# A macaron block (expert feed-forward, state-space mixer, expert feed-forward): named activation table sets, fewer paced scatters, and sums of squares moved from VectorE to ScalarE

## The chip, the cores and the metric

One core of a Trainium2 chip runs the whole kernel as one launch. TensorE multiplies matrices, VectorE, ScalarE and GpSimd (POOL in the profile) work elementwise, SyncE (SP) issues transfers, and GpSimd issues the indirect ones. Each engine runs its own instruction list strictly in order and meets the others at semaphores. The metric is the time of one execution on the device in microseconds, the median of the runs.

## The reference, cut to what matters

```python
x = x + 0.5 * _L0_ffn_ref(_layernorm(x), ...)      # shared expert plus the best 2 of 8 experts
x = x + _L0_attn_ref(_layernorm(x), ...)           # the mixer, below
x = x + 0.5 * _L0_ffn_ref(_layernorm(x), ...)
# in the mixer, x is (4, 1024, 128), D_INNER = 256, 4 heads, 16 states
zxbcdt = x @ in_proj_w.T
xBC = silu(conv4(xBC)); u, Bm, Cm = split(xBC)
Bm = Bm / (norm(Bm) + EPS);  Cm = Cm / (norm(Cm) + EPS)
dt = softplus(dt_raw + dt_bias)
S = 1.0 / (1.0 + dt**2 * A)
w = S * (w - dt * A * ys + dt * Bu);  ys = ys + dt * w;  o = ys . C_t      # scan over tokens
h = x + (y * silu(z)) @ out_proj_w.T
v = mean(h * h);  hn = h * rsqrt(v + EPS) * norm2_w
ffn = silu(hn @ gate_w.T) * (hn @ up_w.T) @ down_w.T
```

## The kernel before, in words

There are 4096 tokens, four sequences of 1024, cut in 8 blocks of 512, two to a sequence. The kernel has three parts. The first feed-forward takes the span up to 230 us, the mixer follows up to about 580 us, and the second feed-forward goes to the end.

A feed-forward norms the tokens, chooses two experts for each, and scatters its rows into one region per expert in HBM (`pool_scatter`, one indirect transfer of 128 rows at a time, 8 for a block, line L716). Then it runs the experts over tiles of 128 rows (`pe_experts` and its partners), and scatters the answers back.

The recurrence of the mixer is turned into decays and rotations: the scan over tokens becomes an exponential of running sums of logarithms (`log_sums`) times sines of running sums of an arctangent (`arctan`, `phase_sums`, `sine_args_c`, `sine_c`), so that chunks of 32 tokens can be multiplied on TensorE (`make_gram`, `state_sum`, `outputs`).

The mixer is software-pipelined by hand. Each engine has a function `body(at)` which lists its steps, and `in_order` calls it for n = -8, -7 and on; `at(-5)` is the block whose number is n - 5, or nothing. One call is a turn here. The order in `body` is the order on the engine; nothing reorders it. On ScalarE (L954 on) a turn before is: `theta` (block k), `hnt_copy`, `root`, `sine_c`, `h_start`, `sine_b`, `inverse_ln`, `inverse_exp`, two `silu_gate`, `c_places`, the third `silu_gate`, `silu_u`, `silu_z`, `silu_bc`, `tm_copy` 0, `silu_z`, `tm_copy` 1, `arctan`, then `zt_copy` (L818 and L820, the normed and transposed input of the next block, which TensorE's `project_dt` waits for), `decays`, `dt_parts`, the two steps of the softplus, `z_norm`, `bc_copy`. An activation function needs its table in ScalarE. [...]

On TensorE a turn goes through `make_gram`, `z_features`, `project_dt`, `outputs` 0 and 1, `down`, `project_bc` (L1752), `outputs` 2 and 3, `bc_features`, `gate_up`, the four-tap projections `project_u` (L1696), `out_project` (L1884), `project_z` and at the end `bc_tokens` (L1763). On GpSimd stand the convolution of B and C (`bc_conv`, L550 to L554), the norms of the input (`norms`, L534 to L543), the product `angle_in` (L642), `log_refs`, the powers of the norms (L559, L616), `h_norm`, `h_add`, and for the first five blocks the scatters of the second feed-forward. The wait that paces them:

```python
if NB <= turn < NB + EARLY and i % 2 == 0:
    pool.wait_ge(scattered, 16 * (turn * 2 * TT + i))
```

So before each second scatter of these blocks GpSimd waits until all scatters so far have landed. The last three blocks' 24 scatters come after the mixer without that wait.

VectorE has, among the rest, `mixed` (L1322 to L1333: adds the mixer's answer, then bn_stats, bn_aggr and two small steps for the mean square of h), `bc_squares` (L1165 to L1167: copy from PSUM, square, sum), `bc_normed` (L1175 to L1177), `log_sums` and `phase_sums` (L1200 to L1212).

## Time and profile before

| | us |
|---|---|
| median of 3 runs | 776.09 (774.16 to 776.84) |
| the profiled execution | 775.01 |
| its span, first to last instruction | 773.0 |
| TensorE busy / clock | 646.7 / 0.925 |
| VectorE busy | 545.1 |
| ScalarE busy | 424.6 |
| GpSimd busy | 520.0 |

The time is the span and about 2 us around it. Busy times are sums over the whole kernel, whose parts have different limits. [...] A timeline gives each instruction's start, its duration, and in brackets how long its engine stood idle before it and what ended that.

### The profile page before, as it was taken

What the parts mean: (1) busy time and instruction counts of PE and PEld (TensorE: products, weight loads), DVE (VectorE), ACT (ScalarE), POOL (GpSimd) and SP (SyncE); (2) the same over time, 40 slices, a digit from 0 to 9 for tenths busy, and PEclk for the clock granted to TensorE, in tenths of its full rate; (3) what the DMA queues carried; (4) which work ended last, traced back from release to release, by engine and by line L of the source; (5) the groups of instructions that cost most, each with busy time, mean ns of one, the idle gap of its engine ahead of it and who ended that gap; (6) DMA issues with size and microseconds to landing.
All of it is one profiled execution on the core that took longest, in us unless ns stands there. A gap on an engine that the chain in (4) does not pass through costs nothing.

```text
span 773.0 us, 13708 instructions
## 1 busy us (share of the span) xinstructions
PE 646.7 (84%) x3768; PEld 476.2 (62%) x3768; DVE 545.1 (71%) x1706; ACT 424.6 (55%) x745; POOL 520.0 (67%) x656
## 2 busy tenths in 40 slices
PE   3378889999935378989999999898986889999991
PEld 2245458989822135656666757576753558988861
DVE  4655756666529668886989899999863556656537
ACT  1122225545414999896999997955212224545535
POOL 3777785666645785895979869786765654666650
PEclk9988999999976678979999999899997999999996
DMA  9511223333233000000000000000000133333218
GB/s 266 166 46 50 80 71 81 90 88 90 65 112 124 0 0 2 0 2 1 1 2 1 2 7 12 18 7 22 26 25 28 46 93 86 87 86 93 73 60 290
DMA packets 49368, 46.34 MB, mean 60 GB/s; under 512 B 8456, under 2 KB 42861, under 8 KB 49296
## 3 DMA queue, kind: packets, MB, share of 16 engines
q1 hardware_dynamic: 40592, 28.54, 13.2%
q0 software_dynamic: 8704, 16.93, 6.7%
q8 instruction: 34, 0.56, 0.3%
q14 instruction: 38, 0.31, 0.1%
HBM read 25.30 MB, written 21.19 MB: 60 GB/s over the span
## 4 chain that ended last, share of the span: by engine, by line
PE 49%; POOL 16%; DVE 13%; issue 10%; ACT 8%; DMA 4%; SPq 0%; DVEq 0%; POOLq 0%; ACTq 0%
POOL xs L716 10%; PE ps_tr L2098 5%; PE ps_tr L1696 4%; PE ps_go L2085 4%; PE ps_go L1696 3%; PE ps_go L2098 2%; DMA xs<-rows,pos 2%; POOL ys L732 2%; PE ps_a L2072 2%; PE ps_a L2074 2%; PE ps_a L2073 2%; PE ps_b L2074 2%; PE ps_go L2046 2%; PE ps_b L2072 2%; PE ps_b L2073 2%
## 5 line engine op out<-in xcount | busy, mean ns | idle before, releaser
L732 POOL DMA_INDIRECT ys<-arena,dest x144 | 140.9, 979 | 87.1 <-issue 65.3
L716 POOL DMA_INDIRECT xs<-rows,pos x128 | 127.2, 993 | 59.1 <-issue 35.8
L1015 ACT ACTIVATE silu_a<-ps_a 128x512 f32<-128x512 f32 x32 | 19.1, 597 | 61.1 <-PE ps_a L2036 59.9
L2098 PE MATMUL ps_tr<-w_down_e,arena 128*128 x384 | 50.7, 275 | 0.0
L1543 DVE TENSOR_TENSOR hid<-silu_a,ps_a 128x512 f32<-128x512 f32 x36 | 24.8, 688 | 33.9 <-ACT silu_a L1035 33.9
L1543 DVE TENSOR_TENSOR hid<-silu_a,ps_b 128x512 f32<-128x512 f32 x36 | 24.8, 688 | 33.4 <-ACT silu_a L1035 33.4
L2098 PEld LDWEIGHTS ps_tr<-w_down_e,arena 128*128 128x128 f32 x384 | 46.7, 192 | 0.0
L1510 DVE TENSOR_TENSOR hid<-silu_a,ps_b 128x512 f32<-128x512 f32 x32 | 21.9, 686 | 35.0 <-PE ps_b L2038 33.1
L1044 ACT ACTIVATE arena<-ps_go 128x512 f32<-128x512 f32 x72 | 42.6, 592 | 2.0 <-PE ps_go L2085 2.0
L2085 PE MATMUL ps_go<-ident,hid 128*128 128x128 f32 x288 | 43.2, 272 | 0.2
L1035 ACT ACTIVATE silu_a<-ps_a 128x512 f32<-128x512 f32 x36 | 21.5, 598 | 37.2 <-PE ps_a L2074 37.2
L1035 ACT ACTIVATE silu_a<-ps_b 128x512 f32<-128x512 f32 x36 | 21.5, 597 | 37.0 <-PE ps_b L2074 37.0
L2085 PEld LDWEIGHTS ps_go<-ident,hid 128*128 128x128 f32 x288 | 35.5, 140 | 10.2 <-DVE hid L1543 0.8
L2046 PEld LDWEIGHTS ps_go<-w_shared_down,hid 128*128 128x128 f32 x256 | 33.0, 203 | 10.1 <-issue 10.1
L1867 PE MATMUL ps_go<-arena,state 128*128 128x128 f32 x128 | 32.1, 335 | 7.8 <-DVE us L1313 6.9
L1027 ACT ACTIVATE xt_hi<-ps_tr 128x256 fp32r<-128x256 f32 x48 | 18.5, 385 | 32.5 <-PE ps_tr L2059 32.5
L1997 PE MATMUL ps_tr<-ident,rows 128*128 128x128 f32 x64 | 13.3, 344 | 27.0 <-DVE rows L1426 20.0
L2046 PE MATMUL ps_go<-w_shared_down,hid 128*128 128x128 f32 x256 | 33.2, 285 | 2.6 <-DVE x L1515 2.6
L1867 PEld LDWEIGHTS ps_go<-arena,state 128*128 128x128 f32 x128 | 22.0, 206 | 20.1 <-issue 14.3
L1696 PE MATMUL ps_go<-arena,w_tap 128*128 128x512 f32 x64 | 33.3, 668 | 0.0
L2072 PE MATMUL ps_a<-up_hi,xt_hi 128*128 x72 | 31.8, 442 | 0.3 <-DVE xt_lo L1528 0.3
L2072 PE MATMUL ps_b<-up_hi,xt_hi 128*128 x72 | 31.2, 434 | 0.0
(368 smaller groups left out, 2025.1 us busy)
## 6 DMA issues: line engine op xcount, KB each, us to landing
arena<-xs SPq DMA_DIRECT2D x144, 65.0 KB, 1.9
rows<-ys SPq DMA_DIRECT2D x8, 512.0 KB, 3.7
arena<-ys SPq DMA_DIRECT2D x8, 512.0 KB, 6.9
ys<-arena,dest POOLq DMA_INDIRECT x144
x<-in_L_attn_x SPq DMA_DIRECT2D x8, 256.0 KB, 4.6
arena<-in_L_ffn_ew SPq DMA_DIRECT2D x4, 512.0 KB, 7.0
xs<-rows,pos POOLq DMA_INDIRECT x128
out<-x SPq DMA_DIRECT2D x8, 256.0 KB, 2.8
```

What stands on the lines that cost most here:

```text
L716: pool.indirect_dma_start(xs, bass.IndirectOffsetOnAxis(pos[:, n, i:i + 1], 0), rows[:, n * TT + i % TT, :], None).then_inc(scattered, 16)
L732: pool.indirect_dma_start(ys, bass.IndirectOffsetOnAxis(dest[:, i:i + 1], 0), y_out[:, p % YRING, j, :], None, bounds_check=2 * TOK - 1, o ...
L1035: act.activation(silu_a[:, p % 2, :].rearrange("p (j h) -> p j h", j=2), ps_pair[p % 2][:, :, 0:HID], ACT.Silu).then_inc(silu_e_done, 1)
L1044: act.activation(hid_t[:, p % 2, :], ps_d, ACT.Copy).then_inc(ht_ready, 1)
L1543: dve.tensor_tensor(hid[:, p % 2, 0, :].rearrange("p (j h) -> p j h", j=2), silu_a[:, p % 2, :].rearrange("p (j h) -> p j h", j=2), ps_pai ...
L1696: r = pe.matmul(target, weights(k), zt[:, shift:shift + BT], start=(k == 0), stop=(k == taps - 1))
L1867: pe.matmul(pb["o"][:, at], state[:, k % 2, p * P:(p + 1) * P], cfs[:, q, k * P:(k + 1) * P], start=True, stop=False)
L2046: r = pe.matmul(ps_d[:, t * P:(t + 1) * P], hid[:, turn % 2, k, t * P:(t + 1) * P], w_shared_down[:, k, :], start=(k == 0), stop=(k == 1))
L2072: pe.matmul(target, xt_hi[:, p % 2, mine], hi, start=True, stop=False)
L2073: pe.matmul(target, xt_hi[:, p % 2, mine], lo, start=False, stop=False)
L2085: r = pe.transpose(ps_d[:, at:at + P], hid[:, p % 2, 0, at:at + P], ident[:, :])
L2098: r = pe.matmul(ps_answers(p)[:, j * P:(j + 1) * P], hid_t[:, p % 2, at:at + P], w_down_e[:, bass.ds(which[2 * p + j], 1), k, :].rearrange ...
```

## The change

- ScalarE: `preload_act_table_set` names two sets. `natural_log_exp_and_others` (it has Exp and Ln) is loaded after `arctan`, ahead of `zt_copy`; `silu_and_others` (it has Silu and Sin) before the sines. `inverse_ln` and `inverse_exp` move up, behind `root`.
- ScalarE gets `h_squares` (four squares of 128x128 with a running sum, behind `c_places`) and `bc_take` (a copy and a square out of PSUM, between the second `silu_z` and `tm_copy` 1). VectorE loses the bn_stats, bn_aggr and two small steps in `mixed`, and the copy and the square in `bc_squares`, and waits for ScalarE instead; GpSimd gets one small step in `tail` and one in `bc_norms`.
- Only the first three blocks of the second feed-forward are paced (PACED = 3); blocks 3 and 4 scatter without the wait.
- VectorE: copies to `ctot` and `turns` and the step for `phase_c` go, as does one small step in `bc_normed`; one wait for its own scan is added in `log_sums`.

```diff
+PACED = 3
@@ pool_mixer_const
-            pool.memset(phase[:, 0, 0:1], 0.0).then_inc(m, 1)
+            pool.wait_ge(col_in, 16)
+            pool.tensor_scalar(phase[:, 0, 0:1], col[:, C_OFFC:C_OFFC + 1], 0.0, None, ALU.add).then_inc(m, 1)
@@ pool_mixer, bc_norms, log_refs, tail, h_add
-                pool.tensor_tensor(bc_n[:, 1, :], bc_n[:, 0, :], half8[:, :], ALU.pow).then_inc(bc_norm_ready, 1)
+                step(pool.tensor_tensor(bc_n[:, 1, :], bc_n[:, 0, :], half8[:, :], ALU.pow))
+                pool.tensor_scalar(bc_n[:, 2, :], bc_n[:, 1, :], RMS_EPS, None, ALU.add).then_inc(bc_norm_ready, 1)
...
-                pool.wait_ge(hmv_ready, SQ * b + q + 1)
-                pool.tensor_tensor(hsm[:, 2, :], hsm[:, 1, :], minus_half[:, 0, :], ALU.pow).then_inc(hr_ready, 1)
+                pool.wait_ge(hsq_ready, SQ * b + q + 1)
+                step(pool.tensor_scalar(hsm[:, 0, :], hsq[:, :], 1.0 / P, RMS_EPS, ALU.mult, ALU.add))
+                pool.tensor_tensor(hsm[:, 1, :], hsm[:, 0, :], minus_half[:, 0, :], ALU.pow).then_inc(hr_ready, 1)
...
-                pool.wait_ge(hmv_ready, n + 1)
+                pool.wait_ge(mix_read, n + 1)
@@ pool_scatter
-                if NB <= turn < NB + EARLY and i % 2 == 0:
+                if NB <= turn < NB + PACED and i % 2 == 0:
@@ act_mixer
+            def bc_take(b, q):
+                n = SQ * b + q
+                act.wait_ge(bct_ps_ready, n + 1)
+                after(act, bcn_ready, n)
+                tokens = pb["bct"][:, 0:2 * TT * DS].rearrange("p (g n) -> p g n", n=DS)
+                act.activation(bc_tm[:, :, :], tokens, ACT.Copy)
+                act.activation(bc_sq[:, :, :], tokens, ACT.Square).then_inc(bc_sq_ready, 1)
+            def h_squares(b, q):
+                n = SQ * b + q
+                act.wait_ge(mix_read, n + 1)
+                after(act, hnt_ps_ready, n)
+                after(act, hr_ready, n)
+                for t in range(TT):
+                    r = act.activation(hn[:, t, :], hb[:, t, :], ACT.Square, accum_out=hsq[:, t:t + 1])
+                r.then_inc(hsq_ready, 1)
+            def exp_ln_set(at):
+                if at(-5) or at(-4):
+                    act.preload_act_table_set("natural_log_exp_and_others")
+            def silu_sin_set(at):
+                if at(-6):
+                    act.preload_act_table_set("silu_and_others")
             def body(at):
                 do(theta, at(-5))
                 do(hnt_copy, at(-8))
                 do(root, at(-5))
+                do(inverse_ln, at(-5))
+                do(inverse_exp, at(-5))
+                silu_sin_set(at)
                 do(sine_c, at(-6))
                 do(h_start, at(-7))
                 do(sine_b, at(-6))
-                do(inverse_ln, at(-5))
-                do(inverse_exp, at(-5))
...
                 do(c_places, at(-6))
+                do(h_squares, at(-7))
                 do(silu_gate, at(-8), 2)
...
                 do(silu_z, at(-5), 1)
+                do(bc_take, at(-5))
                 do(tm_copy, at(-6), 1)
                 do(arctan, at(-5))
+                exp_ln_set(at)
                 do(zt_copy, at(-4))
@@ dve_mixer, bc_squares, bc_normed, log_sums, phase_sums, sine_args_c, mixed
-                dve.wait_ge(bct_ps_ready, n + 1)
-                step(dve.tensor_copy(bc_tm[:, :, :], pb["bct"][:, 0:2 * TT * DS].rearrange("p (g n) -> p g n", n=DS)))
-                step(dve.tensor_tensor(bc_sq[:, :, :], bc_tm[:, :, :], bc_tm[:, :, :], ALU.mult))
+                dve.wait_ge(bc_sq_ready, n + 1)
...
-                step(dve.tensor_scalar(bc_n[:, 2, :], bc_n[:, 1, :], RMS_EPS, None, ALU.add))
...
-                dve.tensor_copy(flat(ctot), chunks(t5)[:, :, CH - 1])
...
+                dve.wait_ge(chunk_logs_ready, n + 1)
...
-                step(dve.tensor_copy(turns[:, 0, :], chunks(t3[q])[:, :, CH - 1]))
...
-                dve.tensor_scalar(phase_c[:, :], phase[:, q, 0:CB], col[:, C_OFFC:C_OFFC + 1], None, ALU.add)
-                step(dve.tensor_scalar(phase_b[:, :], phase[:, q, 0:CB], col[:, C_OFFB:C_OFFB + 1], None, ALU.add))
+                step(dve.tensor_scalar(phase_b[:, :], phase[:, q, 0:CB], 0.25, None, ALU.add))
...
-                dve.wait_ge(mix_read, n + 1)
-                for t in range(TT):
-                    r = dve.bn_stats(hstats[:, t, :], hb[:, t, :])
-                step(r)
-                after(dve, hr_ready, n)
-                for t in range(TT):
-                    r = dve.bn_aggr(hmv[:, t, :], hstats[:, t, :])
-                step(r)
-                step(dve.tensor_tensor(hsm[:, 0, :], hmv[:, :, 0], hmv[:, :, 0], ALU.mult))
-                dve.scalar_tensor_tensor(hsm[:, 1, :], hsm[:, 0, :], RMS_EPS, hmv[:, :, 1], ALU.add, ALU.add).then_inc(hmv_ready, 1)
```

## Rows read from the trace of the kernel before

**Rows 1.** Windows: us, each engine's busy time (instructions), granted clock, DMA share, GB/s.
```profile
245.00:294.00 49.00, 31.59 (x107) 16.85 (x108) 35.28 (x108) 48.32 (x73) 34.29 (x62) 0.73 0.01 3
397.00:432.00 35.00, 35.00 (x205) 23.62 (x204) 32.11 (x79) 33.78 (x55) 30.42 (x43) 1.00 0.01 1
```
**Rows 2.** Groups of ScalarE's table loads (line, count, busy us, mean ns).
```profile
L881 ACT ACT_TABLE_LOAD x8 | 10.3, 1283 | 0.1
...
L861 ACT ACT_TABLE_LOAD x1 | 1.3, 1283 | 0.0
```
**Rows 3.** Chain that ended last, at the mixer's start.
```profile
256.96 1.28 ACT L889
258.25 0.63 ACT arena L889
...
265.45 0.69 ACT arena L820
```
**Rows 4.** GpSimd's timeline in the first turn: convolution, and the product for the arctangent.
```profile
251.27 4.61 POOL L550 TENSOR_SCALAR arena<-bc_raw,col 128x128 f32<-128x128 f32 x4 [0.46 <-ACT bc_raw L842]
...
261.89 1.27 POOL L642 TENSOR_TENSOR arena<-arena 128x512 f32<-128x512 f32 x1
```
**Rows 5.** ScalarE's timeline from the second silu_z to decays, one full turn.
```profile
397.70 0.60 ACT L835 ACTIVATE zs<-ps_tr 128x512 f32<-128x512 f32 x1 [0.37 <-PE ps_tr L1696]
...
398.70 1.28 ACT L905 ACT_TABLE_LOAD   x1
...
401.42 0.69 ACT L820 ACTIVATE arena<-ps_go,col 128x512 f32<-128x512 f32 x1
402.12 1.28 ACT L894 ACT_TABLE_LOAD   x1
...
411.29 0.28 ACT L842 ACTIVATE bc_raw<-ps_b 128x131 f32<-128x131 f32 x1
...
436.21 0.69 ACT L820 ACTIVATE arena<-ps_go,col 128x512 f32<-128x512 f32 x1
```
**Rows 6.** TensorE's timeline: project_dt (w_dt) in three turns, bc_tokens (L1763) in two.
```profile
323.50 0.27 PE L1763 MATMUL ps_b<-ident,bc_silu 128*128 128x128 f32 x1
...
327.83 1.13 PE L1696 MATMUL ps_tr<-arena,w_dt 128*128 128x512 f32 x2 [0.17 <-ACT arena L820]
...
402.26 1.03 PE L1696 MATMUL ps_tr<-arena,w_dt 128*128 128x512 f32 x2
...
437.89 1.02 PE L1696 MATMUL ps_tr<-arena,w_dt 128*128 128x512 f32 x2
...
510.45 0.27 PE L1763 MATMUL ps_b<-ident,bc_silu 128*128 128x128 f32 x1
```
**Rows 7.** TensorE's timeline: the longest idle times inside the mixer.
```profile
303.85 0.46 PE L1867 MATMUL ps_go<-arena,state 128*128 128x128 f32 x2 [2.42 <-DVE us L1313]
...
336.82 0.77 PE L1867 MATMUL ps_go<-arena,state 128*128 128x128 f32 x2 [1.53 <-DVE us L1313]
...
485.95 0.52 PE L1867 MATMUL ps_go<-arena,state 128*128 128x128 f32 x2 [2.26 <-DVE us L1313]
...
565.97 2.92 PE L1931 MATMUL ps_tr<-w_down,arena 128*128 128x128 f32 x24 [1.34 <-DVE state L1302]
```
**Rows 8.** Windows, columns as in rows 1: two stretches at the lower clock.
```profile
305.30:312.10 6.80, 6.57 (x27) 4.27 (x24) 5.48 (x12) 6.72 (x11) 6.64 (x8) 0.50 0.01 4
...
336.00:346.30 10.30, 9.48 (x35) 5.97 (x36) 8.15 (x15) 10.18 (x17) 9.97 (x12) 0.50 0.00 1
```
**Rows 9.** Groups of VectorE instructions, form by form (busy us, mean ns, idle before).
```profile
L1325 DVE BATCH_NORM_STATS2 hstats<-arena 128x6 f32<-128x128 f32 x32 | 7.0, 282 | 0.3
```
**Rows 10.** GpSimd's timeline at the mixer's end.
```profile
574.98 0.96 POOL L716 DMA_INDIRECT xs<-rows,pos  x1 [2.10 <-DMA xs<-rows,pos]
...
595.03 1.04 POOL L706 TENSOR_TENSOR rstd<-var_eps,minus_half 128x4 f32<-128x4 f32 x1
...
603.63 0.96 POOL L716 DMA_INDIRECT xs<-rows,pos  x1 [0.30 <-issue]
```

More of the change, by code:

```diff
@@ L53 @@
 LARGEST = 5e34
[L54 removed]
+C_NORM1, C_NORM2, C_CONVB, C_CONVBC, C_ALOG, C_DTB, C_D, C_OFFC, C_TAPBC = 0, 1, 2, 4, 5, 6, 7, 9, 11
 NCOL = 15
@@ L264, in macaron @@
         refs = sb("refs", [P, TT, CT])
-        turns = sb("turns", [P, 3, CB])
-        phase_c = sb("phase_c", [P, CB])
+        turns = sb("turns", [P, 2, CB])
         phase_b = sb("phase_b", [P, CB])
@@ L275, in macaron @@
         hf = part(1, [P, FC, BT])
-        hmv = sb("hmv", [P, TT, 2])
-        hstats = sb("hstats", [P, TT, 6])
-        hsm = sb("hsm", [P, 3, TT])
+        hsq = sb("hsq", [P, TT])
+        hsm = sb("hsm", [P, 2, TT])
         banks = [pair[:, k, :] for pair in (ps_a, ps_b, ps_go, ps_tr) for k in range(2)]
@@ L376, in macaron @@
         u_ps_ready, z_ps_ready, silu_u_done, silu_z_done = ([sem(f"m_{n}{k}") for k in range(2)] for n in ("u_ps", "z_ps", "silu_u", "silu_z"))
-        (bc_raw_ready, bc_conv_ready, bc_rep_ready, logs_ready, h_added, rep_c_read, rep_b_read, mix_read) = (
-            sem("m_" + n) for n in ("bc_raw", "bc_conv", "bc_rep", "logs", "h_added", "rep_c_read", "rep_b_read", "mix_read"))
+        (bc_raw_ready, bc_conv_ready, bc_sq_ready, bc_rep_ready, logs_ready, h_added, rep_c_read, rep_b_read, mix_read) = (
+            sem("m_" + n) for n in ("bc_raw", "bc_conv", "bc_sq", "bc_rep", "logs", "h_added", "rep_c_read", "rep_b_read", "mix_read"))
         def xt_slot(turn):
@@ L577, in log_refs @@
                 after(pool, bf_ready, n - 1)
-                refs_own.step(pool.tensor_tensor(refs[:, :, :], cinc[:, :, :], ctot[:, :, :], ALU.subtract))
-                refs_own.settle()
-                refs_own.step(pool.tensor_tensor(refs[:, :, :], refs[:, :, :], cmid[:, :, :], ALU.add))
+                refs_own.step(pool.tensor_scalar(refs[:, :, 0:1], cmid[:, :, 0:1], 1.0, 0.0, ALU.mult, ALU.add))
+                refs_own.step(pool.tensor_tensor(refs[:, :, 1:], cinc[:, :, 0:CT - 1], cmid[:, :, 1:], ALU.add))
                 refs_own.settle()
@@ L1201, in phase_sums @@
                                             ALU.mult, ALU.add))
-                step(dve.tensor_copy(turns[:, 0, :], chunks(t3[q])[:, :, CH - 1]))
-                step(dve.tensor_scalar(turns[:, 1, :], turns[:, 0, :], ROUND, -ROUND, ALU.add, ALU.add))
-                step(dve.tensor_tensor(turns[:, 2, :], turns[:, 0, :], turns[:, 1, :], ALU.subtract))
-                start = 0.0
+                ends = chunks(t3[q])[:, :, CH - 1]
+                step(dve.tensor_scalar(turns[:, 0, :], ends, ROUND, -ROUND, ALU.add, ALU.add))
+                step(dve.tensor_tensor(turns[:, 1, :], ends, turns[:, 0, :], ALU.subtract))
+                start = phase[:, 0, 0:1]
                 if q == 1:
@@ L1208, in phase_sums @@
                     dve.tensor_copy(phase[:, 1, 0:1], start)
-                step(dve.tensor_tensor_scan(phase[:, q, 1:], turns[:, 2, :], turns[:, 2, :], start,
+                step(dve.tensor_tensor_scan(phase[:, q, 1:], turns[:, 1, :], turns[:, 1, :], start,
                                             ALU.add, ALU.bypass))
-                dve.tensor_scalar(phase_c[:, :], phase[:, q, 0:CB], col[:, C_OFFC:C_OFFC + 1], None, ALU.add)
-                step(dve.tensor_scalar(phase_b[:, :], phase[:, q, 0:CB], col[:, C_OFFB:C_OFFB + 1], None, ALU.add))
+                step(dve.tensor_scalar(phase_b[:, :], phase[:, q, 0:CB], 0.25, None, ALU.add))
             def sine_args_c(b, q):
@@ L1219, in sine_args_c @@
                 after(dve, cfs_ready, n - 1)
-                step(dve.tensor_tensor(chunks(t6[q]), chunks(t3[q]), spread(phase_c[:, :]), ALU.add))
+                step(dve.tensor_tensor(chunks(t6[q]), chunks(t3[q]), spread(phase[:, q, 0:CB]), ALU.add))
                 dve.tensor_scalar(t7, t6[q], ROUND, -ROUND, ALU.add, ALU.add)
@@ L2251, in laid_out @@
     col[:, C_OFFC] = np.where(part == 0, 0.0, 0.25)
-    col[:, C_OFFB] = np.where(part == 0, 0.25, 0.5)
     arrays["columns"] = col
```

10 lines of the change are left out of this document (4 added, 6 removed).

## The prediction

> **What bounds the kernel now.** I read the windows by stage first. The mixer has two regimes. From 245 to 294 us ScalarE is busy 48.32 of 49.00 us and TensorE only 31.59, at a mean clock of 0.73; from 397 to 432 us TensorE is busy 35.00 of 35.00 us at the full clock, ScalarE 33.78 and VectorE 32.11 [rows 1]. So in the fill ScalarE sets the pace, and in the steady turns TensorE does, with ScalarE and VectorE little behind. The groups of ScalarE come next: table loads of 1.283 us. The mixer has 66 of them in ten groups, of which a full and the smallest are shown [rows 2], and in a full turn there are eight. The chain of the fill runs over them [rows 3]. Then the waits at the hand-overs: TensorE reaches project_dt at the moment at which ScalarE has delivered the next block's input. It idled 0.17 us in the turn of 327.83, and in that of 402.26 ScalarE's L820 ends at 402.11 [rows 5, 6]. Last the end of the mixer, where GpSimd stands 2.10 us before a scatter until the one before has landed [rows 10]. That stretch ends in the last rstd at 595.03, for which VectorE waits.
>
> **Part 1, table loads.** By the sets' names, a full turn needs three loads after the change (silu with sine, arctangent, exponential with logarithm) where it had eight, and the mixer 26 where it had 66. That is 40 x 1.283 = 51 us of ScalarE's time. What of it lies on the path is read stage by stage.
>
> *Fill.* Up to the arctangent's load of the second block, the chain passes 15 loads. One of the five that stay (the first exponential one) moves into idle time ahead of zt_copy. So ScalarE alone would gain 10 x 1.283 = 12.8 us. It does not get that, because others are late next. In the first turn bc_raw comes 2.5 us sooner, and GpSimd then needs from 251.27 to 263.16, 11.9 us, for the convolution, the norms and the product ahead of the arctangent [rows 4]. So the arctangent can begin at 260.7, the new load follows it, and zt_copy of the second block ends at 264.25 instead of 266.14 [rows 3], 1.9 us sooner. In the second turn I get 2.9 us at zt_copy, and 4.9 us at the point where TensorE waited 2.42 us for VectorE's `us` [rows 7]. This wait shrinks to about 1.3 us. If it no longer lowers the clock, the 6.8 us at the lower clock [rows 8] go too and give back half of their length, 3.4 us. h_squares costs 1.3 us here, since it waits for `mixed` ahead of silu_u. I count turns from bc_tokens to bc_tokens: 323.5 us and 510.5 are the first and the last of six, with 362.6, 397.8, 432.6 and 469.1 between [rows 6]. At 323.5 the gain is 7.5 us.
>
> *The turn from 323.5 to 362.6.* It is 39.1 us long. It has 2.7 us of TensorE's idle time, the 1.53 us of rows 7 among it, and 10.3 us at the lower clock [rows 8], worth 4.75 us less the idle part. The rest is 31.7 us of work. To that comes the new idle time of part 2, 1.9 us, and 0.5 us of the old one: 34.2 us, a gain of 4.9.
>
> **Part 2, what the new order adds.** The load of the exponential set stands ahead of zt_copy and not behind it (at 402.12 in [rows 5]), and bc_take is put before tm_copy 1. The load costs 1.30 us with its gap. A copy out of PSUM of this size took 0.28 us alone L842 in [rows 5] and less than that beside its neighbours; its bounds for two passes are 0.3 and 0.6 us, and I take 0.35, near the pace at which such passes follow each other. L820 then ends 1.7 us later after silu_z than now. Queued behind the load are zt_copy and the decays. TensorE waits for the first in project_dt and has nothing else to do, since its list is in order. Where it now arrives just in time, it idles 1.9 us (turns of 294.9, 327.8 and 366.9) or 1.7 us (402.26). In the turns of 437.89 and 474.35 it arrives 0.8 us after the end of L820 at 436.90, so that it idles 0.9 us [rows 5, 6]. In TensorE's regime this is a loss: turns to 397.8, 432.6 and 469.1 us: +1.6, +1.7 and +0.8 us. In the turn from 469.1 to 510.5 the wait of 2.26 us for `us` [rows 7] and its lower clock, worth 3.4 us, go against 0.9 us of new idle time and a rest of 0.3, which is -4.4 us.
>
> h_squares, four passes with a running sum: the trace has no such pass. Lower bound is 4 x 0.28, upper twice that if the sum is read out by an instruction of its own. Either fits in a steady turn, because ScalarE loses 5 x 1.283 = 6.4 us there and gains about 1.8. It waits for `mixed`, and silu_gate 2 and silu_u are queued behind it; TensorE's u projection ends at about the same time as before, so I take 0.
>
> [...] In this trace the load at 256.96 ends at 258.24, and the next pass begins at 258.25 [rows 3]. [...]
>
> **Part 3, VectorE.** Per turn go four bn_stats (4 x 0.28), four bn_aggr, two steps of 0.16, copy and square of B and C, one small step in bc_normed [rows 9], two copies and phase_c: some 3.2 us a turn. On the path, between arctangent and `us`, lie only 0.6 us of these, and the later tm_copy takes 0.35 back. bc_squares now waits for ScalarE, which has the squares ready about when VectorE had them: 0. GpSimd gets 0.6 us a turn, of which 0.3 before h_norm; it has idle time in every steady turn.
>
> **Part 4, scatters.** From 558.7 to 595.0 us GpSimd issues 16 scatters of blocks 3 and 4. Seven waits for a landing lie in it, of about 2.1 us idle where there was nothing between [rows 10]. Unpaced, scatters follow at 0.96 + 0.30 = 1.26 us [rows 10]. Counted through, the last of block 4 starts at 585.7, the rstd at 586.7 to 588, 8 us sooner. VectorE's hid passes then come first: they wait for TensorE, which starts again at 584.8 and would now start at 581. So the next step on VectorE is 5.5 to 7 us sooner. From there TensorE's shared expert and 24 scatters run side by side as now. I take -6.0 us for the tail.
>
> [...] Here the scatter beside the mixer's last work took 0.96 us, like that behind it [rows 10], and I go by that. [...]
>
> **The sum** against the profiled execution's 775.0 us (span 773.0 and 2 us around it, 1.1 below the median): -7.5 -4.9 +1.6 +1.7 +0.8 -4.4 = -12.7 for the mixer up to 510, -6.0 for the tail: 756.3 if the clock never falls behind the new idle times.
>
> **The clock.** It fell after idle times of 2.42, 2.26 and 1.53 with 0.97 before it, but not after 1.34 [rows 7, 8]. The new ones, four of 1.7 to 1.9 us, lie between. I take two falls of 6.8 us, worth 3.4 each: 756.3 + 6.8 = 763.1. With the median's 1.1 us, **764**.
>
> **The rivals.**
> - *The clock holds.* The new idle times are too short for it: 756 to 759. For it: 1.34 us left it alone. Chance 0.2.
> - *The clock falls in nearly each turn*, or the fill gains less because GpSimd or PSUM hand-overs hold it: four or five falls, 756.3 + 13.6 to 17, so 770 to 774. For it: 1.53 us sufficed once, with company. Chance 0.2.
> - *Slower.* Every one of the six new idle times in project_dt lowers the clock for as long as the fall of 10.3 us did, 5.15 us each: 756.3 + 30.9 = 787. It decides from the fourth such fall on, which eats the 18.7 us gained. Against it: two of the six are 0.9 us long. Chance 0.06.
> - *The sets aren't kept*, and the compiler still loads single tables. Then the scatters and some VectorE steps are all: 769. Chance 0.04.
> - The forecast, 760 to 769, with one to three falls: 0.5.
>
> **How the numbers follow.** The range is 756 to 775: it leaves out the slower case and parts of both ends. Below 0.3% (2.3 us, about what a measurement can tell) under 776.1 lie the forecast, the first rival, the fourth and most of the second: faster 0.86. The rest of the second is the same: 0.07. Slower 0.07.
>
> **What would show it.** Right: 26 loads in the mixer; project_dt with an idle time of 1.7 to 1.9 us behind ScalarE's L820 in four turns and about 0.9 in two; steady turns of 36.5 us; the wait for `us` under 0.7 us; scatters of blocks 3 and 4 at 1.26 us; the last rstd 14 to 20 us sooner. Wrong: project_dt without idle time (then bc_take or the load is cheaper than I read), a fill that is shorter by 12 us (then GpSimd was not late next), or scatters that stretch beyond 1.5 us.

## The result, and the profile after

| kernel | median, us | ratio to the kernel before, 95% interval |
|---|---|---|
| before | 776.0 | |
| after | 771.7 | 0.9942 (0.9926 to 0.9959) |

The change is worth 4.3 us, where 12 were forecast (764). All medians are those of the fast runs: left out as slow are two runs of load_twice (790 and 793 us), two of h_add_later's first group, and one of 2206 us each of h_add_later_again and take_and_h_add_again. The profiled execution of the kernel after took 772.2 us with a span of 770.5, against 775.0 and 773.0 before, and the sum of the prediction, made against that execution, gave 763.1. So 9.1 us are to be found.

Windows by stage, columns as in [rows 1] (a granted clock of 1.00 is called the full clock here, one of 0.50 the lower): in both, ScalarE has lost 6 to 7 us of work. In the first, TensorE does more; in the second it is no longer busy from end to end.

```profile
245.00:294.00 49.00, 34.83 (x135) 18.73 (x135) 40.07 (x113) 42.05 (x75) 35.56 (x64) 0.78 0.03 10
397.00:432.00 35.00, 33.50 (x192) 22.01 (x190) 29.79 (x60) 26.88 (x58) 28.84 (x43) 1.00 0.01 1
```

Groups of ScalarE's table loads, which answer to [rows 2]. These are 25; with one for silu_u in the first turn the mixer has 26, as counted ahead.

```profile
L978 ACT ACT_TABLE_LOAD x9 | 11.5, 1283 | 0.2
L914 ACT ACT_TABLE_LOAD x8 | 10.3, 1283 | 0.1
L983 ACT ACT_TABLE_LOAD x8 | 10.3, 1283 | 0.1
```

L978 names `natural_log_exp_and_others`, L983 `silu_and_others`, and L914 is `arctan`. One full turn in ScalarE's timeline, each load 1.28 us: behind the one of L978 at 397.17, six passes with Exp and three with Ln run without another load; behind that of L983 at 413.16, two with Sin and eight with Silu, until `arctan` has one at 431.11. So the first set served Exp and Ln, the second Sin and Silu. The kernel before names no set, and in one of its turns eight loads stand, three of them at a change between Exp and Ln (407.29, 414.03 and 421.93, at L865, L881 and L889).

TensorE's timeline at project_dt (now L1715) and at the first and the last bc_tokens of [rows 6] (now L1782). In brackets stands the idle time ahead and what ended it.

```profile
291.44 1.13 PE L1715 MATMUL ps_tr<-arena,w_dt 128*128 128x512 f32 x2 [1.93 <-ACT arena L820]
...
317.16 0.27 PE L1782 MATMUL ps_b<-ident,bc_silu 128*128 128x128 f32 x1
...
361.40 1.58 PE L1715 MATMUL ps_tr<-arena,w_dt 128*128 128x512 f32 x2 [1.93 <-ACT arena L820]
...
399.44 1.13 PE L1715 MATMUL ps_tr<-arena,w_dt 128*128 128x512 f32 x2 [1.50 <-ACT arena L820]
...
435.99 1.13 PE L1715 MATMUL ps_tr<-arena,w_dt 128*128 128x512 f32 x2 [0.66 <-ACT arena L820]
...
508.43 0.27 PE L1782 MATMUL ps_b<-ident,bc_silu 128*128 128x128 f32 x1
```

All six idle times are there, at the forecast length (1.93, 1.94, 1.93, 1.50, 0.66 and 0.65 against 1.9, 1.9, 1.9, 1.7, 0.9 and 0.9). The turns from 317 to 508 are where the sum goes astray first. Turns from bc_tokens to bc_tokens, from the traces; "again" is a second profiled execution of the same kernel, in another group of runs:

| turn ends in before at | 362.6 | 397.8 | 432.6 | 469.1 | 510.5 | at the lower clock |
|---|---|---|---|---|---|---|
| before | 39.1 | 35.2 | 34.8 | 36.5 | 41.4 | 17.1 us |
| after | 38.2 | 38.0 | 36.6 | 38.0 | 40.5 | 13.7 us |
| after, again | 35.6 | 36.5 | 36.6 | 38.0 | 41.4 | 6.8 us |

What was not forecast at all comes behind them. ScalarE's and then TensorE's timeline of the kernel after, in the emptying pipeline:

```profile
532.75 2.59 ACT L969 ACTIVATE cfx<-xt 32x512 f32<-32x512 f32 x4
538.84 0.31 ACT L949 ACTIVATE silu_a<-arena 128x128 f32<-128x128 f32 x1 [3.50 <-DVE arena L1352]
539.06 0.19 ACT L949 ACTIVATION_READ_ACCUMULATOR silu_a<-arena 128x1 f32 x1
...
540.02 0.57 ACT L958 ACTIVATE arena<-ps_go 96x512 f32<-96x512 f32 x1
```
```profile
536.17 0.59 PE L1863 MATMUL ps_a<-tm 128*128 128x256 f32 x2
540.74 2.04 PE L1843 MATMUL ps_go<-cfx,bf 128*128 128x128 f32 x8 [3.98 <-ACT arena L958]
...
549.74 0.39 PE L1886 MATMUL ps_go<-arena,state 128*128 128x128 f32 x2
```

L949 is h_squares. It waits for VectorE's `mixed` (L1352), and silu_gate 2 (L958) stands behind it on ScalarE, though TensorE had delivered its operand by 535.3. TensorE needs the bank that silu_gate 2 reads (ps_go) and stands 3.98 us. In the kernel before, silu_gate 2 ran right behind c_places, and TensorE went on (ScalarE's and TensorE's timelines):

```profile
534.00 2.57 ACT L949 ACTIVATE cfx<-xt 32x512 f32<-32x512 f32 x4
536.59 0.59 ACT L938 ACTIVATE arena<-ps_go 96x512 f32<-96x512 f32 x1
```
```profile
537.23 0.59 PE L1844 MATMUL ps_a<-tm 128*128 128x256 f32 x2
537.66 1.05 PE L1824 MATMUL ps_go<-cfx,bf 128*128 128x128 f32 x8
...
545.33 0.46 PE L1867 MATMUL ps_go<-arena,state 128*128 128x128 f32 x2
```

In the kernel after the lower clock follows (539.4 to 546.3). TensorE's last product ahead of the wait starts at 537.23 before and at 536.17 after, the output product behind it at 545.33 and at 549.74: 5.5 us are lost in this one place. (Of the 2.0 us won at 508.43, 0.9 had gone by then, most of it at a wait for `gram` of 1.70 us for 1.03.)

GpSimd's timeline at the end, the lines that answer to [rows 10]:

```profile
581.08 0.96 POOL L716 DMA_INDIRECT xs<-rows,pos  x1 [0.30 <-issue]
582.42 1.04 POOL L706 TENSOR_TENSOR rstd<-var_eps,minus_half 128x4 f32<-128x4 f32 x1
...
590.11 0.96 POOL L716 DMA_INDIRECT xs<-rows,pos  x1 [0.30 <-issue]
591.43 1.04 POOL L706 TENSOR_TENSOR rstd<-var_eps,minus_half 128x4 f32<-128x4 f32 x1
598.45 1.09 POOL L716 DMA_INDIRECT xs<-rows,pos  x1 [5.98 <-DVE pos L1492]
```

From 574.63 on the scatters follow each other at 1.26 us, without a wait for a landing. From the rstd at 565.69 to the last one it takes 25.7 us, against 33.7 before (561.35 to 595.03): 8 us less, as counted. But that stretch begins 4.3 us later. And of the 3.6 us by which the last rstd comes sooner, 1.1 are gone by the next scatter (598.45 for 600.97).

### The profile page after: what moved, and what is told of

Read it like the earlier page. It is cut to its first block, busy times and chain, and to the rows that moved or that the text cites. A ratio compares the mean times of both kernels' runs of the same rounds, so it can differ in the third digit from the quotient of the medians.

```text
span 770.5 us, 13635 instructions
## 1 busy us (share of the span) xinstructions
PE 643.7 (84%) x3768; PEld 474.0 (62%) x3768; DVE 529.4 (69%) x1578; ACT 385.1 (50%) x785; POOL 520.5 (68%) x672
## 3 DMA queue, kind: packets, MB, share of 16 engines
q1 hardware_dynamic: 40592, 28.54, 13.3%
## 4 chain that ended last, share of the span: by engine, by line
PE 44%; POOL 24%; issue 13%; DVE 11%; ACT 5%; DMA 2%; POOLq 0%; SPq 0%; ACTq 0%; DVEq 0%
POOL xs L716 9%; POOL ys L732 8%; PE ps_tr L1715 5%; PE ps_go L1715 3%; PE ps_tr L2117 3%; PE ps_go L2104 2%; PE ps_go L2065 2%; PE ps_go L1890 2%; PE ps_go L1886 2%; PE ps_a L2055 2%; PE ps_b L2057 2%; PE ps_tr L1903 1%; PE ps_go L2117 1%; PE ps_go L1843 1%; PE ps_a L2091 1%
## 5 line engine op out<-in xcount | busy, mean ns | idle before, releaser
L716 POOL DMA_INDIRECT xs<-rows,pos x128 | 127.3, 995 | 52.9 <-issue 35.8
L1069 ACT ACTIVATE silu_a<-ps_b 128x512 f32<-128x512 f32 x36 | 21.5, 597 | 37.7 <-PE ps_b L2093 37.7
L1069 ACT ACTIVATE silu_a<-ps_a 128x512 f32<-128x512 f32 x36 | 21.5, 597 | 37.4 <-PE ps_a L2093 37.4
L1715 PE MATMUL ps_go<-arena,w_tap 128*128 128x512 f32 x64 | 31.9, 645 | 0.0
```

Source lines behind the costliest of these rows:

```text
L716: pool.indirect_dma_start(xs, bass.IndirectOffsetOnAxis(pos[:, n, i:i + 1], 0), rows[:, n * TT + i % TT, :], None).then_inc(scattered, 16)
L1069: act.activation(silu_a[:, p % 2, :].rearrange("p (j h) -> p j h", j=2), ps_pair[p % 2][:, :, 0:HID], ACT.Silu).then_inc(silu_e_done, 1)
L1715: r = pe.matmul(target, weights(k), zt[:, shift:shift + BT], start=(k == 0), stop=(k == taps - 1))
```

## Experiments

Each was timed beside the kernel before. The runs of one kernel spread by 1.5 to 11 us, and with TensorE's mean granted clock: six of sets_unpaced gave 759.9 us at 0.942 to 766.0 at 0.926. Over all these kernels, 0.01 of clock goes with 4.1 to 4.4 us inside a kernel's own runs. The last column takes that out, at 4.4 (mean of the runs, each brought to 0.934); there the kernel before comes out at 773.7 to 774.1 in four groups of 11 to 17 runs. The other kernels have 4 to 10 runs each, so that differences of some 2 us can be read, and with both_behind (four runs) only of some 3. What a wait does through the clock is taken out with it.

| kernel | median, us | ratio, 95% interval | at clock 0.934, us |
|---|---|---|---|
| before | 776.0 to 776.6 | | 773.9 |
| after | 771.7 | 0.9942 (0.9926 to 0.9959) | 771.5 |
| after_again | 768.6 | 0.9922 (0.9898 to 0.9947) | 770.7 |
| load_twice | 780.7 | 1.0059 (1.0027 to 1.0091) | 778.2 |
| load_behind | 769.0 | 0.9906 (0.9886 to 0.9926) | 766.9 |
| squares_behind | 765.7 | 0.9863 (0.9838 to 0.9889) | 767.8 |
| both_behind | 764.9 | 0.9854 (0.9835 to 0.9872) | 763.9 |
| before_unpaced | 767.4 | 0.9894 (0.9871 to 0.9917) | 767.3 |
| sets_unpaced | 762.6 | 0.9824 (0.9788 to 0.9859) | 763.0 |
| sets_unpaced_again | 765.3 | 0.9847 (0.9816 to 0.9878) | 763.5 |
| sets_ahead | 763.5 | 0.9833 (0.9805 to 0.9861) | 764.8 |
| sets_all_unpaced | 764.0 | 0.9835 (0.9804 to 0.9866) | 762.9 |
| spare_pass | 770.2 | 0.9939 (0.9910 to 0.9968) | 769.2 |
| squares_on_vector | 762.8 | 0.9825 (0.9794 to 0.9857) | 762.7 |
| steps_on_vector | 765.9 | 0.9849 (0.9821 to 0.9878) | 764.0 |
| h_add_later_again | 758.9 | 0.9776 (0.9750 to 0.9803) | 760.8 |
| take_and_h_add_again | 755.3 | 0.9749 (0.9702 to 0.9796) | 761.5 |

**squares_behind.** h_squares changes places with silu_gate 2.

```diff
-                do(h_squares, at(-7))
                 do(silu_gate, at(-8), 2)
+                do(h_squares, at(-7))
```

> The kernel after, with h_squares behind silu_gate 2 instead of ahead of it. Theory A (in the emptying pipeline silu_gate 2 stands on ScalarE behind h_squares, which waits for VectorE's mixed, and TensorE waits 3.98 us at 536.76 for the bank that silu_gate 2 reads): the wait falls to about 0.8 us, as in the kernel before, the 6.8 us at the lower clock behind it go, and everything from 549.7 on comes 5.4 us sooner: 766 to 767 us. Theory B (VectorE itself is late there, and the place of h_squares doesn't matter): the wait stays above 3 us with another releaser, 771 to 772 us.

Measured 765.7 us: 6.0 under the kernel after and 2.9 under after_again, 3 to 4 at equal clock. Theory A. ScalarE's and TensorE's timelines:

```profile
531.01 0.59 ACT L958 ACTIVATE arena<-ps_go 96x512 f32<-96x512 f32 x1 [0.17 <-PE ps_go L1936]
534.34 0.31 ACT L949 ACTIVATE silu_a<-arena 128x128 f32<-128x128 f32 x1 [2.74 <-DVE arena L1352]
```
```profile
532.10 1.05 PE L1843 MATMUL ps_go<-cfx,bf 128*128 128x128 f32 x8
...
536.14 0.67 PE L1863 MATMUL ps_tr<-tm 128*128 128x256 f32 x2 [1.44 <-ACT tm L933]
```

h_squares still waits, but now only tm_copy is queued behind it, which costs 1.44 us; the clock doesn't fall there. From the last product ahead of this place (531.67) to the output product (540.04) it takes 8.4 us, against 13.6 in the kernel after and 8.1 before: 5.2 us are back.

**load_behind and both_behind.** The load of the exponential set goes behind zt_copy; both_behind has the move of h_squares too.

```diff
-                exp_ln_set(at)
                 do(zt_copy, at(-4))
+                exp_ln_set(at)
```

> The kernel after, with the load of the exponential set behind zt_copy instead of ahead of it. Theory A (TensorE waits in project_dt for zt_copy, and this load is most of that wait): the six idle times there (1.93, 1.94, 1.93, 1.50, 0.66 and 0.65 us) shrink by up to 1.28 us each, to 0.65, 0.65, 0.65, 0.2, 0 and 0, 6.5 us in all, and of the clock's falls behind them (10.2 us at 324.4 and 3.4 us at 361.9) at least one goes, worth 1.7 to 5 us. The time is then 761 to 765 us against 771.7 of the kernel after. Theory B (the load only changes its victim: decays and GpSimd's products behind them come 1.3 us later, and TensorE waits there): 770 to 772 us, with idle times of the same length at the gram or output products.

> The kernel after with both moves: the load behind zt_copy and h_squares behind silu_gate 2. If both waits are separate losses, their gains add up: 6 to 10 us from the first and 5.4 us from the second, 756 to 760 us against 771.7. If GpSimd's scatters in the last turns set the end of the mixer, the second gain swallows part of the first: 762 to 765 us.

Measured 769.0 and 764.9 us. The load's place alone is worth 3.8 to 4.6 us at equal clock (against the two groups of runs of the kernel after) and 3.9 (against squares_behind), h_squares' 3.0 (both_behind to load_behind): within the 3 us that both_behind allows, the two add up. But 769.0 lies above the range of theory A (761 to 765), and 764.9 above the 756 to 760 of the sum; it falls into the other range, whose reason (scatters that set the end of the mixer) was not tested. Of 8.6 us of idle time in project_dt, 1.5 are left in load_behind (0.5 us in three turns). So not all of it had been on the path: the two turns behind 362.6 are 35.8 and 35.6 us long in both kernels, against 36.6 in the kernel after where the clock held, and the next 38.0 and 37.9, against 38.0. Theory A holds for the wait, but not for all of its worth.

**sets_ahead.** The same question with nothing else changed, against sets_unpaced below: the load stands ahead of zt_copy.

> sets_unpaced (762.6 us) with the load of the exponential set ahead of zt_copy, where the change has it; nothing else differs. Theory A (the prediction's: TensorE idles in project_dt by the load's length in the turns that it sets, and nothing later pays that back): idle times of 1.3 to 1.6 us in four turns and 0.3 in two, up to 6 us in all, and one or two falls of the clock more: 767 to 772 us. Theory B (later waits of the same turn shrink by as much, since VectorE and GpSimd are as late as TensorE): 762 to 765 us, and the idle times at the waits for us and gram get shorter.

Measured 763.5 us, where sets_unpaced took 762.6 and 765.3. At equal clock it is 1.3 to 1.8 us. Nearer to theory B. The idle times are there:

```profile
359.02 1.13 PE L1709 MATMUL ps_tr<-arena,w_dt 128*128 128x512 f32 x2 [1.59 <-ACT arena L821]
395.23 1.13 PE L1709 MATMUL ps_tr<-arena,w_dt 128*128 128x512 f32 x2 [1.16 <-ACT arena L821]
```

But the turns are 36.2, 36.2, 37.5 and 42.1 us long against 35.6, 35.6, 39.0 and 40.8: 0.6 us lost twice, 1.5 won back, 1.3 lost. The 1.5 us are the clock's, not a shorter wait's: sets_unpaced has 3.4 us at the lower clock in that turn (446.5), sets_ahead none. And the two turns ahead of these are shorter with the load ahead (31.2 and 38.5 against 33.4 and 39.4), with 10.2 us at the lower clock against 20.4. So the turns of these two executions don't give the load's price; the medians and the time at equal clock do, to about 1.5 us.

**load_twice.** A second load, of the other set and without use, ahead of the first (the kernel after otherwise).

```diff
+            def silu_set_again(at):
+                if at(-4):
+                    act.preload_act_table_set("silu_and_others")
...
+                silu_set_again(at)
                 exp_ln_set(at)
                 do(zt_copy, at(-4))
```

> The kernel after (771.7 us) with a second table load ahead of zt_copy in each turn, 1.28 us each, which does nothing. Theory A (the idle time of TensorE in project_dt takes all of it): the six idle times grow to 3.2, 3.2, 3.2, 2.8, 1.9 and 1.9 us, 7.7 us in all, and the clock falls behind nearly all of them, worth 3.4 us each: 785 to 795 us. Theory B (part of the turns is set by VectorE and GpSimd, so that an idle time of TensorE is half paid back by shorter waits later in the turn, and the clock falls no more often than now): 775 to 780 us. The loss by load_behind (2.7 us for the first 1.28 us each) speaks for B.

Measured 780.7 us, 9.0 over the kernel after (6.7 to 7.6 at equal clock), between the two theories. ScalarE and TensorE:

```profile
291.33 1.28 ACT L983 ACT_TABLE_LOAD   x1
292.62 1.28 ACT L978 ACT_TABLE_LOAD   x1
```
```profile
294.89 1.13 PE L1721 MATMUL ps_tr<-arena,w_dt 128*128 128x512 f32 x2 [3.22 <-ACT arena L820]
...
482.83 1.13 PE L1721 MATMUL ps_tr<-arena,w_dt 128*128 128x512 f32 x2 [1.94 <-ACT arena L820]
```

All six idle times grew by 1.28 us, a load's own length and no more, 7.7 us in all, and nearly all of it is in the time: at these lengths little later in the turn pays it back. The clock fell behind three of the six: for 17.1 us behind 294.89, 3.4 behind 367.56 and 10.2 behind 482.83. Behind the wait of 3.22 us at 331.85 it held (windows):

```profile
331.80:338.00 6.20, 6.15 (x45) 4.02 (x45) 5.07 (x10) 5.69 (x14) 5.92 (x7) 1.00 0.02 4
```

**before_unpaced.** The kernel before with PACED = 3 and nothing else.

> The kernel before with only the scatters of blocks 3 and 4 unpaced. By the prediction's count the last rstd comes 8 us sooner (587 instead of 595.0) and the end 6 us sooner: 770 us. Rival: TensorE's restart at 584.8 hangs on the rstd at 581.9, of which only two landings (4.2 us) lie behind it, and what follows is TensorE's own work, so that no more than 2 to 4 us reach the end: 772 to 774 us. Second rival: unpaced scatters beside VectorE's passes stretch beyond 1.5 us each, and nothing is gained: 776 us.

Measured 767.4 us, below all three expectations: 8.9 us less than the kernel before beside it (776.3), where the whole change brought 4.3, and 7.7 in the group of after_again. At equal clock 6.6, against 2.4 to 3.2: twice what the whole change brings. GpSimd's timeline:

```profile
585.19 0.96 POOL L717 DMA_INDIRECT xs<-rows,pos  x1 [0.30 <-issue]
586.52 1.04 POOL L707 TENSOR_TENSOR rstd<-var_eps,minus_half 128x4 f32<-128x4 f32 x1
592.46 1.09 POOL L717 DMA_INDIRECT xs<-rows,pos  x1 [4.90 <-DVE pos L1474]
```

The last rstd is 8.5 us sooner than at 595.03 [rows 10], and the next scatter as much. The count of the prediction holds (585.7 for the last scatter's start, 585.2 here); that only 6 of its 8 us would reach the end does not. The profiled execution has no stretch at the lower clock in the mixer's end, where the one of the kernel before has 10.2 us (from 581.5 on).

**sets_unpaced.** That kernel and the named sets, the load behind zt_copy. No step changes its engine; inverse_ln and inverse_exp move up on ScalarE, as in the change.

> The kernel before_unpaced (767.4 us) with the named table sets alone, their load behind zt_copy; no step moves from VectorE to ScalarE and none goes. Theory A (the fill's 7.4 us are kept, since the steady turns are TensorE's and gain or lose nothing): 759 to 761 us. Theory B (in the steady turns the sooner passes of GpSimd come to stand beside VectorE's steps and hold them, 1.1 us at a time, so that TensorE waits for gram and us; both_behind showed turns of 35.8, 35.6 and 37.9 us against 35.2, 34.8 and 36.5 of before): turns as long as in both_behind, and 764 to 766 us.

> sets_unpaced beside it on the same chip: 762.6 us again, within 1.5 us, and 2 to 4 us above h_add_later if the held steps cost what they seem to.

Measured 762.6 and again 765.3 us; at equal clock both lie 4 us under before_unpaced, for 40 loads fewer. bc_tokens of the third turn is at 318.0 instead of 323.2 in before_unpaced, and the eighth at 508.5 instead of 510.1: of 5.2 us, 3.6 are given back in the turns between (3.4 us more at the lower clock among it), which is theory B's mechanism; the two times lie in the gap between the theories and in B's range. The second run is 2.7 us off the first, not within 1.5 as expected; at equal clock it is 0.5.

**spare_pass.** sets_unpaced with a pass that nobody needs, on GpSimd, where it stands idle.

```diff
                 pool.tensor_tensor(t1[q], t0[q], t1[q], ALU.add).then_inc(dt_ready, 1)
+                pool.wait_ge(spare_done, n + 1)
+                pool.tensor_tensor(spare[:, :], spare[:, :], spare[:, :], ALU.add).then_inc(spare_done, 1)
```

> sets_unpaced (762.6 us) with one more pass of 128x512 on GpSimd behind dt_sum in each turn, 1.27 us, that computes nothing which is used; GpSimd stands idle there for 2.9 us. Theory A (a pass of GpSimd holds certain short steps of VectorE that begin beside it): VectorE's steps of 0.16 to 0.5 us that fall beside the new pass take 1.1 to 1.3 us more, the turns from 355 to 510 lengthen by 0.5 to 1.3 us each, and the time is 765 to 770 us. Theory B (the long steps have another cause, and GpSimd's idle time swallows the pass): 761 to 764 us, and no step of VectorE is longer beside it.

Measured 770.2 us, 5.7 to 6.2 over sets_unpaced at equal clock. Theory A. VectorE's, GpSimd's and TensorE's timelines at one place:

```profile
481.16 2.74 DVE L1195 TENSOR_SCALAR bc_n<-bc_n 128x8 f32<-128x8 f32 x1
```
```profile
481.60 1.27 POOL L642 TENSOR_TENSOR hid<-hid 128x512 f32<-128x512 f32 x1
482.82 1.04 POOL L646 TENSOR_TENSOR spare<-spare 128x512 f32<-128x512 f32 x1
```
```profile
485.39 0.46 PE L1887 MATMUL ps_go<-arena,state 128*128 128x128 f32 x2 [3.24 <-DVE us L1333]
```

A step of VectorE on 128x8 elements, 0.17 us by itself, lasts until both passes of GpSimd are over (483.86), `us` comes later by that, and TensorE waits. The other turns show it too: TensorE waits 1.13, 0.83 and 3.24 us for `us` (at 371.35, 407.50 and 485.39) where it waits 0.30, 0.26 and 1.67 in sets_unpaced, and 1.09 us for `gram` (at 443.37) where it waits 0.44.

**h_add_later, and take_and_h_add.** The cause taken away: GpSimd's h_add (a pass of 128x512) goes behind bc_spread, in sets_unpaced and in squares_on_vector (below).

```diff
-                do(h_add, at(-5))
                 do(route_scatter, early(at(-9)), 2)
                 do(dt_sum, at(-2))
                 do(bc_spread, at(-3))
+                do(h_add, at(-5))
```

> sets_unpaced (762.6 us) with GpSimd's h_add (128x512, 1.27 to 1.47 us) behind bc_spread instead of ahead of dt_sum, so that one pass less stands beside VectorE's short steps ahead of us. Theory A (GpSimd's passes hold these steps): the steps of 0.95 to 1.6 us at 368, 403, 404 and 439 fall to below 0.7 us or to one, dt_sum comes up to 1.4 us sooner, turns of 35.0 to 35.4 us instead of 35.6, and 38 instead of 39: 758 to 761 us. Theory B (h_add only holds other steps later, us or gram, or delays gated_output): 762 to 766 us.

> h_add_later once more, since its first run was on a chip on which the kernel before took 846.6 us instead of 776, with the loads late ahead of the mixer and in the experts; the turns of the mixer could be read there (34.8, 35.0 and 37.7 us against 35.6, 35.6 and 39.0 of sets_unpaced). If they are as short here: 758 to 761 us. If the time is only moved: 762 to 765 us.

> take_and_h_add once more, for the same reason: 758 to 761 us if VectorE's steps that bc_take and the removed small steps save are on the path, and 1 us or less beside h_add_later if they are not.

In the group of the first runs the kernel before took 846.6 us (h_add_later 824.0 and take_and_h_add 827.4 us; ratios 0.9712, 0.9661 to 0.9762, and 0.9783, 0.9733 to 0.9832). In a group like the others, with sets_unpaced and the kernel after beside them, 758.9 and 755.3 us: 6.4 and 10.0 under sets_unpaced (765.3 there), 1.5 to 2.7 at equal clock, and 9.7 and 13.3 us under the kernel after (768.6 there), the fastest of all. At equal clock the two are alike (760.8 and 761.5); most of what the medians show beyond 2 us is the clock (0.939 and 0.942 in the mean, against 0.932 of sets_unpaced_again). The turns of h_add_later's second execution are 37.4, 34.8, 35.0, 37.7 and 39.6 us; the second and the third, in which neither kernel left the full clock, are 35.6 and 35.6 in sets_unpaced. So 0.6 to 0.8 us a turn are free of the clock. In sets_unpaced, `state` of VectorE stood beside two passes of GpSimd:

```profile
367.98 1.61 DVE L1315 SCALAR_TENSOR_TENSOR state<-state,decay,state_new 128x256 f32<-128x256 f32 x1
```
```profile
366.60 1.48 POOL L634 TENSOR_TENSOR x<-x,arena 128x512 f32<-128x512 f32 x1
368.03 1.27 POOL L639 TENSOR_TENSOR arena<-arena 128x512 f32<-128x512 f32 x1
```

In h_add_later's second execution L639 comes first, with no L634 ahead of it, and is over when `state` begins:

```profile
362.21 0.53 DVE L1315 SCALAR_TENSOR_TENSOR state<-state,decay,state_new 128x256 f32<-128x256 f32 x1
```
```profile
361.18 1.28 POOL L639 TENSOR_TENSOR arena<-arena 128x512 f32<-128x512 f32 x1 [0.33 <-ACT arena L866]
```

**squares_on_vector and steps_on_vector.** both_behind with h's mean square on VectorE again, and with B/C's copy and squares there too.

> both_behind (764.9 us) with h's mean square alone back on VectorE; bc_take stays on ScalarE. Beside steps_on_vector this splits the two. If h_squares relieves VectorE: 766 to 769 us, 1 to 4 us above both_behind. If its wait for mixed costs ScalarE as much as VectorE gains: 764 to 766 us.

> both_behind (764.9 us) with h's mean square and B/C's copy and squares on VectorE, as before the change; the sets, the place of the load, the unpaced scatters and the removed small steps stay. Theory A (what was handed to ScalarE relieves VectorE in the turns in which it is late, 2.3 us a turn of its time): 767 to 771 us. Theory B (the passes on ScalarE add waits across engines that cost what they save): 762 to 765 us.

Measured 762.8 and 765.9 us, against 764.9 of both_behind; at equal clock 762.7, 764.0 and 763.9. The three lie within 1.4 us, too close to say on which engine these steps are better off. That h_squares relieves a late VectorE is not borne out; nor is a gain by bc_take and the removed small steps, since take_and_h_add, which has them, equals h_add_later at equal clock.

**sets_all_unpaced.** PACED = 0 in sets_unpaced.

> sets_unpaced (762.6 us) with the scatters of blocks 0 to 2 unpaced too, that is no wait for a landing at all. Theory A (a wait for a landing of 2 us stands at 550 and holds GpSimd's next passes): the last rstd 1 to 2 us sooner, 760 to 762 us. Theory B (in the turns a scatter is spread over other steps and its landing is past anyway): 762 to 763 us. Theory C (the scatters then stand closer to VectorE's and GpSimd's other steps and hold them): 764 to 766 us.

Measured 764.0 us, at the lower end of theory C, but 762.9 at equal clock, as sets_unpaced (763.0 and 763.5): theory B, no difference. The waits for a landing that count are those of blocks 3 and 4.

**after_again.** The kernel after once more.

> The kernel after on the same chip as the three others, for the difference between kernels without the chip's own: 771.7 us, as before, and so 7 to 12 us above the others. If it comes out below 769, part of the ladder from the kernel after to sets_unpaced was the chip.

Measured 768.6 us, and 770.7 against 771.5 at equal clock: most of the difference is the clock's. By the sign set ahead (below 769), part of the ladder of medians from the kernel after to the others is not the kernels': against this group the steps are 3.1 us smaller than against 771.7. Its profiled execution is the third row of the table of turns; the wait ahead of L1843 is 3.99 us there.

## Why the prediction was right and wrong

The profiled executions differ by 2.5 us of span (2.8 of time); the sum of the prediction had 11.9 (18.7 won less 6.8 for the clock).

| step of the sum | forecast, us | measured, us |
|---|---|---|
| start of the mixer (first L820, 241.47 and 242.54) | 0 | +1.1 |
| fill, to bc_tokens at 323.5 | -7.5 | -7.4 |
| turn to 362.6 | -4.9 | -1.0 |
| turns to 397.8, 432.6, 469.1 | +1.6, +1.7, +0.8 | +2.8, +1.8, +1.6 |
| turn to 510.5 | -4.4 | -0.9 |
| the clock's falls | +6.8 | in the rows above |
| tail | -6.0 | -0.5 |

The 9.4 us between the two sums are 1.1 ahead of the mixer, 0.1 in the fill, 2.7 in the turns when the 6.8 us for the clock are put against them, and 5.5 in the tail.

*Right.* The fill, at its end to 0.1 us: 26 loads, and bc_tokens at 317.16. The idle times in project_dt, their places and lengths. In the kernel after, the steady turns lost what was said (+1.8 for +1.7 where the clock held, 36.6 us for 36.5); the third lost twice that (+1.6 for +0.8). The scatters at 1.26 us and 8 us less between the rstds. Of the signs of being right two failed: the last rstd came 3.6 us sooner and not 14 to 20, and the wait for `us` was 1.02 us at 298.28 and 1.25 at 484.58, not under 0.7.

*Wrong, 5.5 us: the tail.* The step that failed is "silu_gate 2 and silu_u are queued behind it; TensorE's u projection ends at about the same time as before, so I take 0". The waiting instruction and the queue behind it were named, but priced in a full turn, where silu_u and others fill the time. In the emptying pipeline VectorE is late with `mixed`, ScalarE has nothing else, and the only step behind is the one that TensorE needs. Measured: 3.98 us of waiting with 6.8 us at the lower clock behind it, 5.5 us lost in this place, and 5.2 of them back in the trace when the two steps alone are exchanged (2.9 and 6.0 us by the medians, 3 to 4 at equal clock). The unpaced scatters were mis-sized the other way, 8.9 us for 6.0 by the medians (6.6 at equal clock): the guess that VectorE's hid passes and TensorE would swallow 2 us had no row behind it. In the kernel after 1.1 of the 8 us are lost between the last rstd and the next scatter.

*Wrong, 3.5 us: the turn to 510.5.* The wait of 2.26 us did shrink (to 1.25) and the clock held, but the price of the lower clock, 3.4 us, was not on the path. VectorE's timeline shows what was late next, in before and after:

```profile
487.98 2.53 DVE L1473 CAST pos<-pos_f 128x8 uint32<-128x8 f32 x1
490.18 0.67 DVE L1346 TENSOR_TENSOR x<-x,ps_tr 128x512 f32<-128x512 f32 x1
```
```profile
486.61 2.54 DVE L1492 CAST pos<-pos_f 128x8 uint32<-128x8 f32 x1
488.82 0.67 DVE L1365 TENSOR_TENSOR x<-x,ps_tr 128x512 f32<-128x512 f32 x1
```

TensorE's next product waits for that x (1.99 us, at 489.75), which is 1.4 us sooner and no more. In before the slow clock had merely filled that time.

*Wrong in kind: the clock.* Two falls were deduced from the lengths of idle times. The same program with the same idle time (1.94 us in both executions) had 10.2 us at the lower clock behind it in one and 3.4 in the other. First the kernel after, then the same kernel again, windows as in [rows 8]:

```profile
324.40:334.60 10.20, 10.20 (x50) 6.60 (x50) 8.81 (x16) 6.25 (x14) 8.72 (x10) 0.50 0.01 2
```
```profile
322.90:326.30 3.40, 3.40 (x14) 2.12 (x14) 2.52 (x5) 2.98 (x7) 3.40 (x5) 0.50 0.00 0
326.30:333.10 6.80, 6.54 (x56) 4.42 (x56) 6.61 (x13) 5.29 (x11) 6.56 (x6) 1.00 0.02 4
```

In the first execution the turns from 323.5 on held 13.7 us at the lower clock, as the two falls of 6.8 forecast, and in the second 6.8: that the term came out in the first is luck. Its price was off too. The sum takes half of the length, 3.4 us for 6.8. The same turns of the same program, to 362.6 and to 397.8, are 38.2 and 38.0 us long with 10.2 and 3.4 us at the lower clock, and 35.6 and 36.5 with 3.4 and none: 2.5 us for 6.8 and 1.5 for 3.4, about 0.4 of the length. The runs' slope gives less still: 0.01 of clock is 15 us at the lower level in a span of 773, for 4.1 to 4.4 us, an estimate of 0.3. A part of what TensorE loses at the lower clock it would else have spent waiting, as in the turn to 510.5.

So the clock is a spread of some us on every kernel here and not a term that can be assigned to one idle time; in load_twice, waits of 3.22 us each were followed by 17.1 us at the lower clock, by 3.4 us and by none. The +1.1 us ahead of the mixer are spread too: the second execution of the same program began it at 241.07.

*Not seen: what the fill's gain turned into.* With the sets alone, project_dt undelayed and no step on another engine, the steady turns are 35.6, 35.6 and 39.0 us (3.4 at the lower clock in the last) against 35.2, 34.8 and 36.5. When ScalarE delivers sooner, GpSimd's h_add and dt_sum come sooner too and stand beside VectorE's short steps ahead of `us` (rows above); spare_pass adds such a pass and costs 6 us at equal clock, h_add_later takes one away there and wins 2.2 to 2.7. The prediction had the idle times of GpSimd as harmless ("it has idle time in every steady turn"). The load ahead of zt_copy costs less than TensorE's idle time (1.3 to 1.8 us at equal clock for 6.1 us of it in sets_ahead, 3.8 to 4.6 for 7.1 in the kernel after against load_behind); that it moves these passes back again would explain it, but was not tested.

The rivals: the time of the second, 770 to 774, came out, but for another reason than its four or five falls. The slower case needed four falls of 10.3 us; one of that length came (324.4).

## What to carry to other kernels

When a step that waits for another engine is put into an in-order queue, price it in each stage of the pipeline, above all in the emptying one, where nothing else fills the wait and the next instruction in the queue may be the one that frees a bank: here the exchange of two lines gave back 5 us in the trace (3 to 6 by the medians), beside a change that brought 4.3. Where an engine speeds up, look at the passes that it triggers on GpSimd, and at which short steps of VectorE they will then stand beside; idle time of GpSimd doesn't make them free (spare_pass, a pass put where it stood idle, cost 5.7 to 6.2 us at equal clock). And try the smallest edit by itself: PACED = 3 alone gave twice what the whole change gave, and with the named sets and h_add moved the kernel takes 758.9 us.
